# The rounding constant of the gated values on ScalarE, one chunk more under way, the last chunk in halves

## The reference

```python
def fp4_quant_dequant(x):
    xb = x.reshape(shape[:-1] + (shape[-1] // BLOCK, BLOCK))        # BLOCK = 16
    scale = jnp.max(jnp.abs(xb), axis=-1, keepdims=True) / 6.0
    scale = jnp.maximum(scale, jnp.float32(1e-12))
    xn = xb / scale
    q = _GRID[jnp.searchsorted(_MID, jnp.abs(xn))] * jnp.sign(xn) * scale
...
x = x + fp4_linear(silu(fp4_linear(n, w_gate)) * fp4_linear(n, w_up), w_down)    # n = x, gate 128 -> 352 -> 128
```

## Time and profile before

| | us |
|---|---|
| median of three runs | 2228.53 |
| the profiled execution | 2224.48 |
| its span | 2222.7 |
| last stage, from the first Silu to the end of the span | 2079.4 to 2222.7 |
| DVE, ACT, POOL busy over the whole span | 1625.4, 1343.4, 1103.8 |
| TensorE busy, mean granted clock | 1986.2, 0.958 |

### The profile page before, as it was taken

The page is one execution under the profiler, slowest core; times in us unless marked ns, Lnnn a source line. Parts: engine busy times, 40 slices in busy tenths (PEclk is TensorE's granted clock), DMA queues, the critical chain, the costliest instruction groups (busy, mean ns, idle before and its releaser), DMA issues. The chain is left out here.

```text
span 2222.7 us, 56156 instructions
## 1 busy us (share of the span) xinstructions
PE 1986.2 (89%) x17787; PEld 1008.8 (45%) x17787; DVE 1625.4 (73%) x3434; ACT 1343.4 (60%) x2148; POOL 1103.8 (50%) x994
## 2 busy tenths in 40 slices
PE   4789999999999999996599969999999999999765
PEld 3434444444444444445244424444444444444444
DVE  4978888888888888867677776566666566667896
ACT  2246666666666666653355547777877777778421
POOL 1412222233222222334254438777877778778565
PEclk8879999999999999996799989999999999999998
DMA  5622211222221112200012340111111111110000
GB/s 131 186 57 53 50 50 50 53 53 53 52 52 50 50 50 52 53 20 1 1 39 85 105 133 30 39 33 29 43 29 29 43 29 29 43 29 2 0 15 24
DMA packets 127055, 107.09 MB, mean 48 GB/s; under 512 B 39636, under 2 KB 102724, under 8 KB 126956
## 3 DMA queue, kind: packets, MB, share of 16 engines
q1 hardware_dynamic: 120544, 99.83, 16.9%
q10 hardware_dynamic: 6412, 6.18, 1.0%
HBM read 76.01 MB, written 29.53 MB: 47 GB/s over the span
## 5 line engine op out<-in xcount | busy, mean ns | idle before, releaser
L1099 DVE TENSOR_REDUCE b_mx<-psum 128x1 f32<-128x512 f32 x1024 | 663.9, 686 | 142.3 <-PE psum L916 78.2
L1083 ACT ACTIVATE b_prob<-psum 128x1024 f32<-128x1024 f32 x512 | 524.4, 1024 | 320.9 <-PE psum L948 320.8
L1922 POOL TENSOR_TENSOR combT<-attn,f_phi 128x512 f16<-128x512 f32 x512 | 586.9, 1157 | 177.5 <-ACT f_phi L2056 149.7
L2077 DVE TENSOR_REDUCE f_mx<-psum 128x1 f32<-128x512 f32 x512 | 328.6, 683 | 166.6 <-PE psum L1946 166.2
L2055 ACT ACTIVATE attn<-psum 128x512 f32<-128x512 f32 x512 | 308.0, 601 | 172.3 <-PE psum L1957 163.1
L996 PE MATMUL psum<-b_prob,combT 128*32 128x256 f32 x4096 | 328.8, 393 | 1.5 <-ACT b_prob L1083 0.5
L852 POOL COPY combT<-v 128x64 f32 (+1 forms) x64 | 15.7, 246 | 607.9 <-PE psum L996 598.3
L2056 ACT ACTIVATE f_phi<-psum 128x512 f16<-128x512 f32 x512 | 306.2, 598 | 0.0
L948 PE MATMUL psum<-x,b_toep 128*128 128x79 f16 (+1 forms) x4224 | 267.7, 208 | 0.0
L855 POOL TENSOR_TENSOR x<-flip,grev 128x1024 f16<-128x1024 f16 x128 | 240.6, 1901 | 0.0
L948 PEld LDWEIGHTS psum<-x,b_toep 128*128 128x128 f16 x4224 | 236.2, 99 | 9.2 <-issue 2.6
(11 more groups left out here) (322 smaller groups left out, 3390.7 us busy)
## 6 DMA issues: line engine op xcount, KB each, us to landing
f_qk<-d_qk SPq DMA_DIRECT2D x192, 128.0 KB, 2.9
d_qk<-e_qk SPq DMA_DIRECT2D x64, 256.0 KB, 2.6
b_toep<-d_line SPq DMA_DIRECT2D x128, 64.0 KB
b_q<-d_q SPq DMA_DIRECT2D x128, 54.0 KB
d_k<-a_qk SPq DMA_DIRECT2D x48, 128.0 KB, 2.3
b_toep<-d_line SPq DMA_DIRECT2D x128, 32.0 KB
b_q<-b_m SPq DMA_DIRECT2D x256, 1.0 KB
b_q<-d_q SPq DMA_DIRECT2D x128, 27.0 KB
```

Of the source, the lines that this page charges most:

```text
L1083: nc.scalar.activation(prob[:, t % 4, :].rearrange("p (a n) -> p a n", a=2), ps[:, EXP + 2 * (t % 2):EXP + 2 * (t % 2) + 2, :], ACT.Exp).t ...
L1099: nc.vector.tensor_reduce(mx[:, b, t, half:half + 1], ps[:, bank, :], AX.X, ALU.max).then_inc(s.max_read, 1)
L1922: nc.gpsimd.tensor_tensor(plo[:, t % 4, at], prob[:, t % 4, at], phi[:, t % 4, at], ALU.subtract).then_inc(s.plo_ready, 1)
L2077: nc.vector.tensor_reduce(mx[:, b, t, half:half + 1], ps[:, bank + half, :], AX.X, ALU.max).then_inc(s.max_read, 1)
```

## The change

1. DVE's `quant_h` ends with the bitwise and. ScalarE forms the constant in place, in a new stage `magnitude(s-3)`, last in its step: Relu(c - 1), then Identity(MAGIC * c + MAGIC), each over 128x1408 floats with a bias operand in SBUF, the second waiting for the first.
2. `quantise_add` becomes a DVE stage of its own, `round_h(s-4)`, which waits for ScalarE.
3. `add_out`, `down` and `move_hT` run one step later (s-5) and stand first in their engines' steps (on DVE after `stats`); `round_h` follows `add_out`.
4. Chunk 7: all four `hidden` after `quant_h(6)`; its quantisation is done wholly on DVE in two halves of 128x704, and `down`, `move_hT`, `add_out` and the store run by halves.

```diff
+def quantise_ratio(v, src, blocks, t, link):
...
+        nc.vector.memset(q.fixed[:, 0:1], -1.0)
+        nc.vector.memset(q.fixed[:, 1:2], MAGIC)
...
+        def magnitude(n, u):
+            if is_last(n):
+                return
+            act.wait_ge(s.hchain, EARLY * EARLY_LINKS + RATIO_LINKS * (n + 1))
+            nc.scalar.activation(th[u].c, th[u].c, ACT.Relu, bias=s.fixed[:, 0:1]).then_inc(before.rl_ready, 1)
+            act.wait_ge(before.rl_ready, ATTENDED + 2 * n + 1)
+            nc.scalar.activation(th[u].c, th[u].c, ACT.Identity, bias=s.fixed[:, 1:2], scale=MAGIC).then_inc(before.rl_ready, 1)
...
-        pipeline(act, [(2, gates), (4, move_hT), (1, move_xT)])
+        pipeline(act, [(5, move_hT), (2, gates), (1, move_xT), (3, magnitude)])
...
-        pipeline(pe, [(2, gate_up), (4, down), (1, turn_x)])
+        pipeline(pe, [(5, down), (2, gate_up), (1, turn_x)])
...
+        def quant_last(n, u):
+            th2 = CT // 2 * FI
+            dve.wait_ge(s.hid_ready, done(CT * n + CT - 1))
+            link = chain(dve, s.hchain, EARLY * EARLY_LINKS + RATIO_LINKS * n)
+            for half in range(2):
+                v = u ^ half
+                dve.wait_ge(s.hq_ready, done(n + half - 2))
+                dve.wait_ge(s.h_turned, done(F3 * (n + half - 2) + F3 - 1))
...
+            link(quantise_ratio(nc.vector, hid[:, u, :, :].rearrange("p t e -> p (t e)"), CT * FI // QB, th[u], link))
+            link(nc.vector.tensor_scalar(th[u].c.bitcast(U32), th[u].y.bitcast(U32), EXPONENT, None, ALU.bitwise_and))
+        def round_h(n, u):
+            if is_last(n):
+                return
+            dve.wait_ge(before.rl_ready, ATTENDED + 2 * n + 2)
             quantise_add(nc.vector, CT * FI // QB, th[u]).then_inc(s.hq_begun, 1)
...
-        pipeline(dve, [(0, stats), (2, lambda n, u: hidden(n, u, range(2))), (1, quant_x),
-                       (2, lambda n, u: hidden(n, u, range(2, CT))), (3, quant_h), (4, add_out)])
+        pipeline(dve, [(0, stats), (5, add_out), (4, round_h), (2, hidden_part(range(2), False)), (1, quant_x),
+                       (2, hidden_part(range(2, CT), False)), (3, quant_h), (2, hidden_part(range(CT), True))])
```

More of the change, by code:

```diff
@@ L2278, in phase_quant_ffn @@
     out_t = out.rearrange("b (t p) e -> p (b t) e", p=P)
+    ATTENDED = before.units_added
     is_early = lambda n: isinstance(n, int) and n < EARLY
     is_first = lambda n: isinstance(n, int) and n == 0
+    is_last = lambda n: isinstance(n, int) and n == NC - 1
     @block.sync
@@ L2284, in store @@
         def store(n, u):
+            if is_last(n):
+                for half in range(2):
+                    sp.wait_ge(s.y_ready, done(n + half))
+                    at = slice(n * CT + 2 * half, n * CT + 2 * half + 2)
+                    sp.dma_start(out_t[:, at, :], y[:, (u ^ half) * CT:(u ^ half) * CT + 2, :]).then_inc(stored[u ^ half], 16)
+                return
             sp.wait_ge(s.y_ready, done(n))
@@ L2337, in gates, with move_hT @@
                 nc.scalar.activation(silu[:, k % 2, :], ps[:, GU + 2 * (k % 2), 0:FI], ACT.Silu).then_inc(s.silu_ready, 1)
-        def move_hT(n, u):
+        def magnitude(n, u):
+            if is_last(n):
+                return
+            act.wait_ge(s.hchain, EARLY * EARLY_LINKS + RATIO_LINKS * (n + 1))
+            nc.scalar.activation(th[u].c, th[u].c, ACT.Relu, bias=s.fixed[:, 0:1]).then_inc(before.rl_ready, 1)
+            act.wait_ge(before.rl_ready, ATTENDED + 2 * n + 1)
+            nc.scalar.activation(th[u].c, th[u].c, ACT.Identity, bias=s.fixed[:, 1:2], scale=MAGIC).then_inc(before.rl_ready, 1)
+        def move_hT(n, u, width=CHUNK):
+            if is_last(n) and width == CHUNK:
+                for half in range(2):
+                    move_hT(n + half, u ^ half, CHUNK // 2)
+                return
             for c, (x, y_) in enumerate(FC):
@@ L2373, in gate_up, with down @@
                 nc.tensor.matmul(ps[:, bank + 1, 0:FI], x, g.wguT[:, 1, :], start=True, stop=True).then_inc(s.up_psum, 1)
-        def down(n, u):
-            pe.wait_ge(s.hq_ready, done(n))
+        def down(n, u, tiles=CT):
+            if is_last(n) and tiles == CT:
+                for half in range(2):
+                    down(n + half, u ^ half, CT // 2)
+                return
+            if tiles == CT:
+                pe.wait_ge(s.hq_ready, done(n))
+            else:
+                pe.wait_ge(s.nchain, n + 2)
             if is_first(n):
@@ L2383, in down @@
                 pe.wait_ge(s.hT_ready, done(j - 2))
-                for k in range(CT):
+                for k in range(tiles):
                     last = nc.tensor.transpose(ps[0:y_ - x, TH + (F3 * u + c) % 2, k * P:(k + 1) * P], hq[:, u, k, x:y_], g.ident[:, :])
@@ L2430, in quant_h @@
+            link(nc.vector.tensor_scalar(th[u].c.bitcast(U32), th[u].y.bitcast(U32), EXPONENT, None, ALU.bitwise_and))
+        def round_h(n, u):
+            if is_last(n):
+                return
+            dve.wait_ge(before.rl_ready, ATTENDED + 2 * n + 2)
             quantise_add(nc.vector, CT * FI // QB, th[u]).then_inc(s.hq_begun, 1)
         def add_out(n, u):
+            if is_last(n):
+                for half in range(2):
+                    v, at = u ^ half, n * CT + 2 * half
+                    dve.wait_ge(s.out_psum, done(n + half))
+                    dve.wait_ge(stored[v], 16 + (n + half - v) * 8)
+                    nc.vector.tensor_tensor(y[:, v * CT:v * CT + 2, :], g.x[:, at:at + 2, :], ps[:, OUT, 0:2 * P].rearrange("p (t e) -> p t e", t=2), ALU.add).then_inc(s.y_ready, 1)
+                return
```

30 lines of the change are left out of this document (21 added, 9 removed).

## The result

The changed kernel takes 2290.23 us (median of four runs, 2288.28 to 2331.26) against 2232.28 for the kernel before on the same chip (four runs, 2224.49 to 2239.15). The ratio is 1.0269, 95% interval 1.0235 to 1.0303: slower. Its profiled execution took 2290.97 us, span 2289.2.

A forecast was written before the change was run, and what follows sets the result against it. DVE's list bounded the kernel before; the change closes a chain through three lists, 23.5 us a step against 17.07. Start +2.0, chunks 0 to 5 +33.8, end +2.4 and clock +8 on 2224.5 gave 2270 us, range 2250 to 2290.

The forecast's parts named there:

- I take two in five: +8.: Products on the last stage's chain: two in five of seven run at TensorE's lower clock, adding 8 us.
- Rival 1: Low TensorE clock in every step's product: 2283 us, up to 2290 where gate_up is low too; chance 0.2.
- rival 2: ScalarE changes its function table between Relu and Silu: 2280 us with one load on the chain, 2288 with both; chance 0.06.
- the 0.5 for "both": Each step: DVE colliding with POOL, and magnitude standing behind move_xT, 0.5 us together.
- Collisions: DVE and POOL instructions shifted against each other: one or two more collide per step, 0 to 2 us.
- it starts 8.3 later: At the end: chunk 7's second half on DVE waits for finish_h(6), 6.6 us, and the turning of chunk 6, 1.7.
- halving saves less than it gives back: At the end, with chunk 7 in halves: 41.0 us against 38.65 before, +2.4.
- Rivals 3 and 4: 3: chain hides, DVE stays the bound, 2215 us, chance 0.04; 4: only magnitude's wait counts, 2226, no change, chance 0.03.
- contained: DVE's saved 0.92 us a step brings no further gain in the sum, since DVE is idle in each new step.

The follow-up runs named there:

- e8: The changed kernel with add_out last on DVE, gate_up ahead of down on TensorE, gates ahead of the copies on ScalarE; ratio to before 1.0109, stage 151.8 us.
- e1: The changed kernel with one move in ScalarE's list, the copies of down (move_hT) ahead of magnitude; ratio to before 1.0139, stage 164.8 us.
- e3: The changed kernel with dummy products on TensorE after gate_up of chunks 3 to 6 and between transpose groups; ratio to before 1.0173, stage 174.5 us.
- e2: The changed kernel with the constant formed by DVE as before, lists and halves kept; ratio to before 1.0172, stage 163.4 us.
- e6: The changed kernel rebuilt: round_h after quant_x, add_out last, gate_up and gates of two tiles a step earlier, finish_h a step later; ratio to before 1.0016.
- e9: The rebuilt version up to chunk 5, with constant and rounding of chunks 6 and 7 on DVE and no halves; 2224.05 us, ratio to before 0.9962.
- e10: The rebuilt version with chunks 6 and 7 on DVE, no halves, and DVE instead of POOL finishing tiles 2 and 3 of chunk 7; ratio to before 0.9998.

## Why the prediction was right or wrong

The direction (slower) and the mechanism were right: the chain bitwise and, constant, copies, product, `add_out` is in the traces as forecast, and e8 and e1 show it to be the cause of the greater part of the loss, 35.3 of the stage's 62.1 us. The time was not: 2270 was said, and 2290.23 lies 0.2 us above the range of 2250 to 2290. The stage grew by 62.1 us where 46.2 were forecast; the miss is in these terms.

*The step.* From the end of one `round_h` (2131.91) to the next (2159.30), by the terms of the prediction's sum:

| | forecast | measured | difference |
|---|---|---|---|
| rest of DVE's step, to the end of the bitwise and | 12.8 + 0.5 | 14.06 | +0.8 |
| to the end of the second activation | 3.0 | 3.92 | +0.9 |
| to the start of the product | 2.08 | 2.28 | +0.2 |
| product, to `add_out` | 2.94 | 4.90 | +2.0 |
| `add_out` and `round_h` | 2.2 | 2.23 | 0 |
| sum | 23.5 | 27.39 | +3.9 |

*The clock is the term that failed.* "I take two in five: +8." All seven products of 24 in the changed kernel run for the most part at the low level (4.57 to 5.49), and behind the 10.85 us of idleness `turn_x` and the transposes are slow as well. e3 gives the price: up to 2.8 us a step, about what the prediction had for a slow product (2.55 + 0.35), 13.2 over the five steps and 1.6 up to `round_h(6)`, some 15 in place of 8. Rival 1, with a chance of 0.2, was the case, but its price of +20 for seven is more than that: the last of the seven, chunk 6's, lies beside DVE's second half. That its 2290 came out is partly luck, since collisions and the time ahead of the stage, below, filled the rest. The sum took "some 7 us" of idleness before `turn_x`, though its own figures (23.5, less 12 of work, less 2.5) leave 9. It took one row of a product at full speed as evidence, but before that row TensorE had stood 1.42, 0.31 and 0.75 us, where the changed kernel has 10.85, 2.31 and 0.67 in a full step. The trace before also has a product at full speed behind a long idleness (TensorE's timeline, chunk 6):

```profile
2205.47 2.88 PE L2385 MATMUL psum<-square,wT 128*128 128x128 f32 x12 [11.91 <-POOL wT L2320]
2209.02 2.94 PE L2391 MATMUL psum<-wdT,v 128*128 128x128 f32 x24 [0.67 <-ACT v L2345]
```

The changed kernel's own chunk 6 takes 4.81 behind 12.10 us of idleness and 2.87 of transposes, so such an idleness does not tell the level. The other six have a pause more between the transposes, 2.31 in a full step, and all are low; in e1, without that pause, they come at both levels.

*The constant.* 1.47 each against 1.44: right, and no table load (rival 2 fell). The Trainium skill (ScalarE: Activation LUTs, "Table sets: the hidden batching unit") has relu, copy and identity in every set; the trace agrees, with the one load of the last stage, at its first Silu, as before. What was undersized is that it starts 0.95 us after the bitwise and, since `move_xT` is ahead of it in the list and `turn_x` is slow; the 0.5 for "both" was to cover this and the collisions.

*Collisions.* 0.8 a step more than the 0.5 allowed for: the bitwise and takes 1.63 instead of 0.89, beside POOL's L646, which takes 2.32 instead of the 1.06 that the same line had in the earlier trace rows. The prediction allowed for one or two more per step, 0 to 2 us; that is what came, in a place it did not name.

*Start.* +2.1 (E0 to the first `round_h` 4.66 against 2.58), 2.0 forecast.

*Chunks 0 to 5.* 135.3 us against 83.7: +51.6, with 33.8 and 5.7 of the clock's 8 forecast; short by 12.1. e3 ascribes 7.5 of them to the clock (13.2 less 5.7); the rest is left for the collisions and what of the constant's late start is not the slow `turn_x`.

*End.* +8.4 against 2.4 and 2.3 of clock. DVE's first half took 9.15 us (from 2261.76 to 2270.91) and POOL's `finish_h(6)` 9.7 in place of 6.6: each slowed the other, DVE's L646 took 1.36 in the first half and 0.89 in the second, where POOL was silent. The turning of chunk 6 took 2.9 instead of 1.7. So the second half started 12.8 after `round_h(6)`, 8.3 were forecast. This step, "it starts 8.3 later", failed too: it took POOL's price from a stretch in which other instructions of DVE ran beside it. It makes 4.5 of the 6.1 by which the end exceeds its 41.0, and 1.4 came before `round_h(6)`. Taken for the halves alone, "halving saves less than it gives back" was wrong: against the same order without halves (e4) the stage is 9.9 shorter. The end as a whole is still longer than before.

*Ahead of the stage.* 4.9 us of the 66.5 came before E0, in code that did not change but for two one-column memsets. E0 also moved by 17 us between the other kernels, so this need not be an effect of the edit. Without it the profiled execution would have been 2286, inside the range, and the clock term as wrong as now. The prediction worked from one execution 0.2% below the median that it had (0.35% below that of the four runs above); leaving that out made the range too narrow on its upper side.

Rivals 3 and 4 fell: `add_out` waits 9.8 us in each step. That DVE's 0.92 a step is "contained" in idle time agrees with e1 and e2, whose stages are within 1.4 of each other with and without it; their products at the low clock fall in different steps, so the two do not show it to a tenth.

## What to carry to other kernels

Work moved to another engine is paid by its place in that engine's list: follow, from the end of its input, what each in-order list has next, and look for a chain that comes back to the first engine within one step. When a forecast makes TensorE idle longer, work the sum out with its low-clock durations in every step that waits for it, and let the range hold that sum: here the share could not be read from a row or two. Judge a deeper pipeline by its two ends as well: in e6 the 7.7 us won over five steps were lost again at the start and the end. Before a gain of a few microseconds is put down to an edit, look at two executions of the same code.

## What the runs showed of the hardware

- Products were at the low level once TensorE had stood 10.85 and then 2.31 us (4.86), at full speed with filler in both gaps (2.94), and at either (4.66, 2.94) behind 10.86 and 10.85 us without the second gap. Filling the gaps with useless work made the last stage shorter by 12.6 us.
- DVE and POOL: the bitwise and over 128x1408 took 0.89, 1.36, 1.50 or 1.63 us by what POOL did beside it, and POOL's 128x512 multiplication 1.06 or 2.32. At the end both engines lose: DVE's L646 over 128x704 takes 1.36 beside POOL and 0.89 alone, POOL's two groups of four 4.51 and 5.24 where the earlier trace rows has 3.59 and 3.02. The Trainium skill (SBUF — State Buffer, "SBUF: two separate sides") has an exclusive lock on the port pair of the two; the rows agree in that instructions of both become longer, and the order in which they took it was not tried.
- Relu and Identity beside Silu caused no table load in any run.
- The start of the last stage moved by 17 us between executions of nearly the same code ahead of it, more than many differences studied here. The stage moves less, but it moves: e9 and e10 have the same code for the first five steps and took 80.9 and 76.0 us.
